# A graph network's relation products as 32-row matmuls per head, with type masks on VectorE and one transpose a tile

## The reference

```python
def typed_linear(x, types, W):              # x @ W[type of the node]
def typed_linear_heads(xe, types, W):       # per head: xe[e,h,:] @ W[h, type of the edge]
k, q, v = (typed_linear(x, ntype, W).reshape(n, H, HD) for W in (Wk, Wq, Wv))
kw = typed_linear_heads(k[src], etype, att)
a = jnp.sum(kw * q[dst], axis=-1) * pri[:, etype].T / sqrt(HD)
w = softmax of a over the edges of one dst
m = typed_linear_heads(v[src], etype, msg) * w[:, :, None]
h = jax.ops.segment_sum(m, dst, num_segments=n).reshape(n, D)
h = typed_linear(h, ntype, Wa)
return h * alpha + x * (1 - alpha)          # alpha = sigmoid(skip)[ntype]
```

## Time and profile before

| | us |
|---|---|
| timed runs, median of 3 (10056.95, 10076.78, 10077.42) | 10076.78 |
| span of the profiled execution, first to last instruction | 7482.8 |
| the profiled execution's own time | not given |
| PE busy in the span | 5247.3 (70%) |
| DVE (VectorE) busy | 4677.7 (63%) |
| POOL (GpSimd) busy | 4574.3 (61%) |
| ACT (ScalarE) busy | 4061.0 (54%) |

### The profile page before, as it was taken

The page is one execution under the profiler, slowest core; times in us unless marked ns, Lnnn a source line. Parts: engine busy times, 40 slices in busy tenths (PEclk is TensorE's granted clock), DMA queues, the critical chain, the costliest instruction groups (busy, mean ns, idle before and its releaser), DMA issues.

```text
span 7482.8 us, 147503 instructions
## 1 busy us (share of the span) xinstructions
PE 5247.3 (70%) x33354; PEld 4436.1 (59%) x33355; DVE 4677.7 (63%) x12884; ACT 4061.0 (54%) x10084; POOL 4574.3 (61%) x4672
## 2 busy tenths in 40 slices
PE   3966666689666666986666669766666696666664
PEld 2755555567555555765555557566555575565553
DVE  5257777732677777237777752477777425777774
ACT  0346666633566665336666643366666334666662
POOL 0267777641777775337777752477777426777763
PEclk8978888799788887987787889777888897888877
DMA  1333333313333332233333313333333033333331
GB/s 37 160 124 105 104 104 104 92 51 159 109 104 104 104 104 67 93 148 105 104 104 105 105 39 135 134 104 104 104 104 104 28 161 116 104 104 102 102 94 35
DMA packets 272656, 761.00 MB, mean 102 GB/s; under 512 B 87871, under 2 KB 104356, under 8 KB 271908
## 3 DMA queue, kind: packets, MB, share of 16 engines
q0 software_dynamic: 199680, 545.53, 25.2%
q1 hardware_dynamic: 72228, 208.51, 7.1%
HBM read 557.87 MB, written 195.88 MB: 101 GB/s over the span
## 4 chain that ended last, share of the span: by engine, by line
PE 28%; issue 20%; POOL 17%; DVEq 13%; DVE 11%; DMA 5%; POOLq 5%; ACT 1%; ACTq 0%; SPq 0%
POOL rows L446 17%; PE ps L538 8%; DMA rows<-table,idx_now 5%; PE ps L555 4%; DVEq L1066 4%; POOLq L462 4%; DVEq L1056 4%; PE ps L646 3%; PE ps L651 3%; PE ps L558 2%; PE ps L630 2%; DVEq L229 1%; PE ps L521 1%; PE ps L645 1%; DVE wmsg L1032 1%
## 5 line engine op out<-in xcount | busy, mean ns | idle before, releaser
L446 POOL DMA_INDIRECT rows<-table,idx_now x4160 | 4025.4, 968 | 1270.0 <-issue 1151.8
L707 ACT ACTIVATE prod<-iota_n,dloc 128x128 bf16<-128x128 f32 x6240 | 1989.0, 389 | 109.1 <-issue 81.8
L645 PE MATMUL ps<-zeros,identb 128*128 128x132 bf16 x2080 | 522.2, 251 | 1581.8 <-DVE wmsg L1032 1319.7
L630 PE MATMUL ps<-qn,ohT 128*128 x8320 | 1493.1, 335 | 90.9 <-issue 53.4
L630 PEld LDWEIGHTS ps<-qn,ohT 128*128 128x128 f32 x8320 | 1310.5, 240 | 176.7 <-issue 161.0
L645 PEld LDWEIGHTS ps<-zeros,identb 128*128 128x128 bf16 x2080 | 227.7, 109 | 1759.8 <-issue 1664.0
L646 PE MATMUL ps<-wmsg,ohf 128*128 128x132 f32 x4160 | 1141.1, 364 | 0.0
L712 ACT ACTIVATE ohf<-prod,ones 128x512 f32<-128x512 bf16 x1040 | 750.7, 722 | 703.5 <-PE ps L651 617.5
L1050 DVE TENSOR_TENSOR prod<-ps,rows 128x512 f32<-128x512 f32 x1040 | 715.9, 688 | 561.9 <-DMA rows<-table,idx_now 458.4
L651 PE MATMUL ps<-wmsg,ohf 128*128 128x132 f32 x4160 | 992.0, 328 | 0.0
L1028 DVE TENSOR_TENSOR wmsg<-rows,weight 128x512 f32<-128x512 f32 x1040 | 721.1, 693 | 367.1 <-issue 330.6
(11 more groups left out here) (163 smaller groups left out, 6344.6 us busy)
## 6 DMA issues: line engine op xcount, KB each, us to landing
table<-rows SPq DMA_DIRECT2D x245, 768.0 KB, 3.2
rows<-table,idx_now POOLq DMA_INDIRECT x4160
out<-h SPq DMA_DIRECT2D x1, 3072.0 KB
wk<-in_L_gnn_Wk SPq DMA_DIRECT2D x20, 48.0 KB
wq<-in_L_gnn_Wq SPq DMA_DIRECT2D x20, 48.0 KB
wv<-in_L_gnn_Wv SPq DMA_DIRECT2D x20, 48.0 KB
wa<-in_L_gnn_Wa SPq DMA_DIRECT2D x20, 48.0 KB, 2.0
attw<-in_L_gnn_rel_att SPq DMA_DIRECT2D x20, 24.0 KB
```

The costliest lines, as they stand in the source:

```text
L446: pool.indirect_dma_start(out=rows[:, slot, j, :], out_offset=None, in_=table, in_offset=bass.IndirectOffsetOnAxis(ap=idx_now[:, half, c:c ...
L630: last = pe.matmul(ps[:, 2 + b, j * P:(j + 1) * P], ohT[:, b, j, :], qn[:, at(ts[j]), :].rearrange("p a c -> p (a c)"), start=True, stop=True)
L645: pe.matmul(bank[:, AW:2 * AW], identb[:], zeros[:], start=True, stop=True)
L707: act.activation(squares[:, turn % 2, j * P:(j + 1) * P], iota_n[:], ACT.Square, bias=dloc[:, at(4 * q + j)], scale=-1.0)
```

## The change

- The relation products are made per head: `attw` and `msgw` shrink to 32 rows a head and 6 x 32 columns, and eight matmuls of 32 rows and 192 columns write one PSUM bank a head. VectorE now takes heads 0 and 1 of both halves (k times pri, v copied), ScalarE copies heads 2 and 3 of both, and GpSimd then multiplies heads 2 and 3 of k by pri in SBUF. The store waits for that.
- One transpose a tile of the unmasked rows. In the projection GpSimd only stages the tile (a copy that permutes columns), and VectorE makes the three masked copies out of PSUM, with `type_row`, the node types broadcast to all partitions by DMA: once before the first projection and in the output stages.
- In the output stage GpSimd divides one tile by the denominator while it stages it. PE makes one matmul with 384 columns, all three types at once, and VectorE adds the three pieces to h, each times `share` = mask times alpha, with a drain between them.
- ScalarE copies q.

The diff without declarations of semaphores and buffers:

```diff
+            def types_load():
+                whole = (TILES - 1) * P
+                sp.dma_start(type_row[:, 0:whole].bitcast(I32),
+                             ntype[0:whole].rearrange("(o n) -> o n", o=1).broadcast_to((P, whole))
+                             ).then_inc(s_types, 16)
...
+            def output_(l):
+                if not isinstance(l, int):
+                    types_load()
             def project_(l, later):
+                if not later:
+                    types_load()
                 def body(t, b, pair):
-                    hold(sp, s_tabk, l * TILES + t + 1)
-                    hold(sp, s_tabv, l * TILES + t + 1)
+                    hold(sp, s_tab01, l * TILES + t + 1)
+                    hold(sp, s_tabk23, l * TILES + t + 1)
@@ gpsimd: output_, project_
+                hold(pool, s_hn, l + 1)
...
-                    masked(acc[:, at(t), 0:D].rearrange("p a c -> p (a c)"), t, b)
+                    pool.tensor_tensor(staged[:, b, :]..., acc[:, at(t), 0:D]..., rden[:, at(t), :]..., ALU.mult)
                     pool.drain().then_inc(s_hm, 1)
...
+                def scaled(t, b):
+                    hold(pool, s_tab23, l * TILES + t + 1)
+                    k23 = tab[:, b, :, 2 * HD:4 * HD].rearrange("p e (h c) -> p h e c", h=2)
+                    pool.tensor_tensor(k23, k23, priw[:, 2:4, :]...broadcast_to((P, 2, ET, HD)), ALU.mult)
+                    pool.drain().then_inc(s_tabk23, 1)
                 def body(t, b, pair):
                     if not is_first(t, 2):
                         hold(pool, s_tr, tr_base(l, 0) + t - 1)
-                    masked(h[:, at(t), :].rearrange("p a b -> p (a b)"), t, b)
+                    pool.tensor_copy(staged[:, b, :].rearrange("p (r i) -> p r i", r=R4),
+                                     h[:, at(t), :].rearrange("p a (i r) -> p r (a i)", r=R4))
                     pool.drain().then_inc(s_hm, 1)
+                    if not is_first(t, 2):
+                        scaled(t - 2, b)
+                    if is_last(t, TILES):
+                        scaled(t - 1, 1 - b)
+                        scaled(t, b)
@@ tensor: project_, output_
-                    for t3 in range(NT):
-                        last = pe.transpose(ps[:, b, t3 * P:(t3 + 1) * P], hm[:, b, t3, :], ident[:])
-                    last.then_inc(s_tr, 1)
+                    pe.transpose(ps[:, b, 0:P], staged[:, b, :], ident[:]).then_inc(s_tr, 1)
...
-                        for k in range(2):
-                            last = pe.matmul(ps[:, 4 + 2 * a + k, 0:3 * D], kvT[:, o, a, :],
-                                             w[:, 3 * k:3 * k + 3, :].rearrange("p e c -> p (e c)"),
+                        for hh in range(H):
+                            last = pe.matmul(ps[:, 4 + hh, a * ET * HD:(a + 1) * ET * HD],
+                                             kvT[HD * hh:HD * hh + HD, o, a, :],
+                                             w[HD * hh:HD * hh + HD, :, :].rearrange("p e c -> p (e c)"),
                                              start=True, stop=True)
...
-                    for t3 in range(NT):
-                        last = pe.matmul(ps[:, 2 + b, 0:D], hmT[:, b, t3, :], wa[:, t3, :],
-                                         start=(t3 == 0), stop=(t3 == NT - 1))
-                    last.then_inc(s_g, 1)
+                    pe.matmul(ps[:, 2 + b, 0:NT * D], aggT[:, b, :], wa[:].rearrange("p t c -> p (t c)"),
+                              start=True, stop=True).then_inc(s_g, 1)
@@ scalar: project_ (turned is gone), output_
-                    act.copy(tab[:, b, :, D:ROW]..., ps[:, 6:8, 0:3 * D]...).then_inc(s_tabv, 1)
+                    for a in range(2):
+                        last = act.copy(tab[:, b, :, a * D + 2 * HD:a * D + 4 * HD]...,
+                                        ps[:, 6:8, a * ET * HD:(a + 1) * ET * HD]...)
+                    last.then_inc(s_tab23, 1)
...
                     act.copy(kvT[:, b].rearrange("p a c -> p (a c)"), ps[:, 2 + b, 0:2 * P]).then_inc(s_kvT, 1)
+                    act.copy(qn[:, at(t), :].rearrange("p a c -> p (a c)"),
+                             ps[:, 2 + b, 2 * P:3 * P]).then_inc(s_qn, 1)
@@ vector: project_, output_
+                def masked(t, b):
+                    dve.wait_ge(s_tr, tr_base(l, 0) + t + 1)
+                    if not is_first(t, 2):
+                        dve.wait_ge(s_kvq, l * TILES + t - 1)
+                    types = type_row[:, at(t * P, P)].bitcast(I32)
+                    for t3 in range(NT):
+                        last = dve.scalar_tensor_tensor(out=hmT[:, b, t3, :], in0=types, scalar=float(t3),
+                                                        in1=ps[:, b, 0:P], op0=ALU.is_equal, op1=ALU.mult)
+                    last.then_inc(s_hmT, 1)
                 def k_half(t, b, pair):
...
+                    dve.tensor_tensor(tab[:, b, :, 0:2 * HD]..., ps[:, 4:6, 0:ET * HD]..., priw[:, 0:2, :]..., ALU.mult)
+                    dve.tensor_copy(tab[:, b, :, D:D + 2 * HD]..., ps[:, 4:6, ET * HD:2 * ET * HD]...).then_inc(s_tab01, 1)
                 def body(t, b, pair):
+                    if is_first(t):
+                        masked(0, 0)
+                    if not is_last(t, TILES):
+                        masked(t + 1, 1 - b)
...
+                dve.tensor_tensor(share, tmask[:], alpha[:, at(l), :]..., ALU.mult)
                 dve.drain()
                 dve.reciprocal(rden, rden)
-                dve.drain()
-                for a in range(0, TILES, TN):
...
+                dve.drain().then_inc(s_hn, 1)
...
+                    for t3 in range(NT):
+                        last = dve.scalar_tensor_tensor(out=hrow, in0=ps[:, 2 + b, t3 * D:(t3 + 1) * D],
+                                                        scalar=share[:, at(t), t3:t3 + 1].rearrange("p a b -> p (a b)"),
+                                                        in1=hrow, op0=ALU.mult, op1=ALU.add)
+                        if t3 < NT - 1:
+                            dve.drain()
+                    last.then_inc(s_h, 1)
```

More of the change, by code:

```diff
@@ L111, in gnn @@
         wa = sb("wa", [P, NT, D])
-        attw = sb("attw", [P, ET, D])
-        msgw = sb("msgw", [P, ET, D])
+        attw = sb("attw", [P, ET, HD])
+        msgw = sb("msgw", [P, ET, HD])
         priw = sb("priw", [P, H, ET])
@@ L350, in weights @@
                                      d[at(l), :, r:D:R4, :].rearrange("l t i o -> (l i) t o")).then_inc(s_w, 16)
[L351 to L354, removed]
+                for hh in range(H):
+                    a, b = HD * hh, HD * hh + HD
+                    for w, d in ((attw, att), (msgw, msg)):
+                        sp.dma_start(w[a:b, :, :],
                                      d[at(l), hh, :, :, :].rearrange("l t i o -> (l i) t o")).then_inc(s_w, 16)
@@ L395, in last @@
                 sp.wait_ge(s_out, 32)
-            layers(sp, edges_, lambda l: None, project_, last)
+            layers(sp, edges_, output_, project_, last)
         @block.gpsimd
@@ L452, in output_ @@
             def output_(l):
+                hold(pool, s_hn, l + 1)
                 def body(t, b, pair):
[L454 to L457, removed]
                     if not is_first(t, 2):
                         hold(pool, s_tr, tr_base(l, 1) + t - 1)
-                    masked(acc[:, at(t), 0:D].rearrange("p a c -> p (a c)"), t, b)
+                    pool.tensor_tensor(staged[:, b, :].rearrange("p (r h c) -> p h c r", r=R4, h=H),
+                                       acc[:, at(t), 0:D].rearrange("p a (h c r) -> p (a h) c r", h=H, r=R4),
+                                       rden[:, at(t), :].rearrange("p a (h c r) -> p (a h) c r", c=1, r=1
+                                                                   ).broadcast_to((P, H, HD // R4, R4)), ALU.mult)
                     pool.drain().then_inc(s_hm, 1)
@@ L567, in output_, with go @@
             def output_(l):
-                go = turn(l, 1)
+                def go(t, b):
+                    if not is_first(t, 2):
+                        pe.wait_ge(s_hmT, tr_base(l, 1) + t - 1)
+                    pe.wait_ge(s_hm, tr_base(l, 1) + t + 1)
+                    pe.transpose(ps[:, b, 0:P], staged[:, b, :], ident[:]).then_inc(s_tr, 1)
                 def body(t, b, pair):
@@ L663, in _ @@
         def _(act):
[L664 to L671, removed]
             def project_(l, later):
-                turned = copied(l, 0)
                 def v_half(t, b, pair):
@@ L695, in body, with output_ @@
                         v_half(t, b, pair)
+                tiles(act, body)
+            def output_(l):
+                def body(t, b, pair):
+                    act.wait_ge(s_tr, tr_base(l, 1) + t + 1)
+                    if not is_first(t, 2):
+                        act.wait_ge(s_g, l * TILES + t - 1)
+                    act.copy(aggT[:, b, :], ps[:, b, 0:P]).then_inc(s_hmT, 1)
                 tiles(act, body)
@@ L745, in last @@
```

(9 more changed lines are left out.)

90 lines of the change are left out of this document (37 added, 53 removed).

## The result

The changed kernel takes 10670.7 us (median of 4, 10655.8 to 10690.7) against 10077.1 us before: 1.0596 times, interval 1.0577 to 1.0616, or 594 us slower. The forecast was 768 slower. One of the four runs of the kernel before was slow (10813.6 us), and the ratio leaves it out.

A forecast was written before the change was run, and what follows sets the result against it. It took PE to bound the projection and a PE–GpSimd ring to bound it after the change; 10076.78 + 791 + 12 - 35 gave 10845 us. The main case ranged from 10600 to 11050, the 8-in-10 range up to 11250.

The forecast's parts named there:

- The ring: Projection: PE's next transpose waits for GpSimd staging, queued behind scaling that needs PE's last products; 3.25 us a tile.
- rival 4: Projection: cheaper GpSimd scaling and full overlap bring PE's wait path below 2.16 us; faster, 9990 us; chance 0.05.
- The relation products: Projection: eight 32-row matmuls a tile, paced by 16 weight loads of 0.112 us, take 1.8 us instead of 2.58.
- rival 1: Projection: products of all four heads overlap wholly, 0.64 us; 10490 us, or 10320 at full clock; chance 0.20.
- The clock: Projection: PE's granted clock falls from 0.99 to 0.80, taken from the edges, because PE pauses in every tile.
- my formula: Projection tile: PE's work over its clock, plus 3.25 us of waiting; 3.92 / 0.80 = 4.90, so 8.15 us.
- The sum: Whole kernel: projection +791, types' load +12 and output stage -35 us make +768, so 10845 us.
- The types' load: Start of layer 0's projection: VectorE's first mask waits for 3 MB of broadcast types; +12 us.
- The output stage: Output stage: VectorE ready some 8 us earlier, same tile pace; -35 us in all, stages of 85 to 93 us.
- The edges: Edge stage, not touched by the change: some 1105 us a layer, unchanged within 1%.
- 2 (no overlap): Projection: the eight products do not overlap at all, 2.58 us; tile 9.12 us, 11083 us; chance 0.17.
- 3 (the clock falls to 0.59): Projection: ring present and PE's clock as at the output's start, 0.59; tile 9.9 us, 11270 us; chance 0.10.

The follow-up runs named there:

- e1: The changed kernel with GpSimd scaling k three tiles behind its staging instead of two; 9345.5 us, 0.9432 times before.
- e4: The changed kernel with four unread f32 matmuls put ahead of PE's wait in each projection tile; 10222.3 us, 1.0152 times before.
- the pair: The kernel before and the changed kernel, both unchanged, run again on one chip; 10054.3 us and 10654.4 us, 0.9993 and 1.0589 times before.
- e3: The kernel before with the 32-row relation products alone, VectorE scaling heads 2 and 3 of k; 9436.4 us, 0.9523 times before.
- e5: The kernel of e1 with relation products ordered k and v head by head, instead of all k then all v; 9505.8 us, 0.9443 times before.

## Why the prediction was right, and where it was off

**The ring: right.** PE's first instruction of a tile waits for GpSimd's drain behind staging, in every tile, and moving one GpSimd operation by one tile takes the wait away (e1). Link by link the forecast was 3.09 us. The trace has 2.80: the products' end to ScalarE 0.08 (312.72 to 312.80) for 0.17, the copies 0.86 for 0.86, to GpSimd 0.18 for 0.29, the multiply 0.83 for 1.02, drain and issue 0.35 for 0.34, staging 0.40 for 0.30, to PE 0.10 for 0.11. The multiply by a factor that is constant along 32 elements is cheaper than the mask with its permutation, though far from enough for rival 4.

**The relation products: mis-sized.** I took 1.8 us from the pace of the loads, 0.112 each. They take 0.87 at full clock in e1, a third of the 2.58 of the earlier trace rows. The 16 loads run inside them. A single 32-row load has a record as long as a full one's (185 against 190 ns), yet the 16 take 0.64 us in all (302.04 to 302.68 in e4), 0.04 each where I took 0.112. So loads into different row groups overlap more than the nearest rows, loads that all fill 128 rows, could show. The Trainium skill's figure of 3.07 (TensorE: Matmul & The Clock Gate, Part 3), which I set beside the sum at 0.84 us, is near the 2.97 measured (2.58 / 0.87). The Trainium skill's sentence that a load is paid by columns agrees with the single record and is no bound across groups. The Trainium skill (TensorEngine Tiling (Array Packing), Key Properties) says that different tiles can load and multiply in parallel, and this case's trace agrees. The sum should have used 0.87, which is between my forecast and rival 1.

**The clock: mis-sized the other way.** 0.80 from the edges was too high; the stage had 0.72. The that I took it from were of the quick execution: in all others the edges themselves have 0.68. At PE's own 0.11 + 2.01 + 0.87 = 2.99 us and 0.72 my formula would give 4.15 + 3.25 = 7.4 us a tile; the trace has 8.02. A stage's mean clock says little about the clock while PE works. In the tile shown, windows of PE at work on k, v and q and of its pause, with columns as in the earlier trace rows:

```profile
308.00:312.00 4.00, 4.00 (x23) 3.77 (x27) 0.68 (x3) 0.24 (x1) 0.00 (x0) 0.57 0.48 197
312.00:315.00 3.00, 0.72 (x16) 0.43 (x12) 1.02 (x2) 1.16 (x4) 0.83 (x1) 1.00 0.00 0
```

k, v and q ran almost wholly at 1.2 GHz, 3.55 us for 2.01, and the stage's mean of 0.72 also counts the pauses. Over the 40 tiles in 200 to 530 us the granted clock is 0.56 while k, v and q run and 0.93 in the pauses. e4 prices it: 429 us of 2001. Of the 8.02 us a tile, 2.89 are the wait and 5.13 PE's own 2.99 us of work, where I had 3.25 and 4.90. That the tile came out so near 8.15 is luck: the work was overrated, the clock under which it runs was overrated too, and the two errors cancelled.

**The sum.** +791 for the projection was +735 (2001 - 1266). The steady tiles differ by 8.02 - 4.92 = 3.10 us, near the forecast 3.23. I multiplied a steady tile's difference by 245, but the stages' starts and ends don't grow with it: over whole stages a tile is 1266 / 245 = 5.17 us before and 2001 / 245 = 8.17 after, 3.00 apart. The types' load: forecast +12, and the trace has VectorE waiting 9.25 us for it once, while the stage of layer 0 starts 3 us earlier (160.8 for 163.8). The output stage: forecast -35, measured -65. VectorE's rows of the changed kernel there:

```profile
2170.05 0.36 DVE L947 TENSOR_SCALAR rows<-acc 128x196 f32<-128x196 f32 x1 [0.42 <-DVEq L262]
2181.86 1.21 DVE L962 SCALAR_TENSOR_TENSOR h<-ps,rows,h 128x128 f32<-128x128 f32 x3 [2.90 <-PE ps L596]
2183.35 1.20 DVE L962 SCALAR_TENSOR_TENSOR h<-ps,rows,h 128x128 f32<-128x128 f32 x3 [0.29 <-PE ps L596]
2186.21 5.64 DVE L962 SCALAR_TENSOR_TENSOR h<-ps,rows,h 128x128 f32<-128x128 f32 x15 [0.16 <-PE ps L596]
```

The first add comes 11.8 us after the stage's first instruction (2170.05 to 2181.86), where it was 18.1 before (1519.01 to 1537.06): 6 us, near my 8. The 49 tiles behind it take 68 us to the end at 2249.7, 1.38 each, where they took 74 before (1537 to 1611), 1.51 each. I had both at 1.40. That is right of the new stage (1.49 a tile at first, then five tiles in 5.64 us, 1.38 on average). Of the old one it is the steady pace only, and its first tiles, at a clock of 0.59, take longer. That is the other 6 us, and it makes the new stage 80 us long, below the 85 to 93 that I gave as a sign.

The edges: forecast unchanged within 1%, and the pair has -0.6%.

**The rivals.** 1 (products wholly overlapped) was nearly right of the products (0.87 us for its 0.64) and wrong of the total, since it kept the clock at 0.80 or 1.00. 2 (no overlap) fell in e1 and e3. 3 (the clock falls to 0.59) was right of the clock while PE works (2.99 us of work in 5.13, as at 0.58) and had too much work under it. The two together, 2.76 / 0.59 + 3.25 = 7.9 us a tile, come nearest to how the 8.02 are made. 4, the faster side, fell by its own number: the way from PE's last product to the next transpose is 2.80 us, not under 2.16.

**What the change is without the ring.** e1 is the changed kernel with one operation a tile later, 0.9432 times before. The parts of the change were good for -385 (products), -30 to -42 (transposes) and -65 us (output); one place in one engine's queue cost 1150 (2001 - 851).

## What to carry to other kernels

When an operation moves to another engine, read that engine's queue behind it: a wait for the producer's last result, placed ahead of an input that the producer needs first, ties both engines into a ring, and everything that ran ahead stops. Such a ring shows as the producer waiting, in every tile, for an operation that has nothing to do with the wait in front of it, and delaying the waiting operation by one more tile can be the whole cure. Price a pause of TensorE twice, once as time and once through the clock of the work behind it.

## What the runs showed that I had not expected

- One execution of a kernel can have edge stages of 1105 us where all others have 1562 to 1630: same instructions, gathers that take as long each, but without the long waits for something that the profile doesn't name. A span far below the timed runs asks for a second profile before its stages are compared.
- Matmuls nobody reads, put into a pause, saved 431 us (e4).
- Four 32-row groups keep up their overlap in either order of issue (e5).
